# A residual of conditioned 1x1 products whose transfers move one 16 KB run per channel instead of two of 8 KB

## The reference

```python
x                 # (64, 128, 2048) float32: batch, channel, time
itok_B_0_15       # (64,) int32, 0..15
L0_cond_weights   # (16, 128, 128) float32: state, channel, feature

W = weights[condition]
return x + jnp.einsum('bct,bcd->bdt', x, W)
```

## Time and profile before

| | |
|---|---|
| median of three runs | 325.06 us |
| the profiled execution, its own time | 324.97 us |
| its span, from the first to the last instruction | 323.2 us |
| PE, DVE, POOL busy | 240.3, 146.6, 19.0 us |
| moved by DMA | 135.30 MB, 419 GB/s over the span |
| granted TensorE clock, mean | 0.928 |

### The profile page before, as it was taken

One profiled execution on the slowest core, in us unless ns is written; L12 is line 12 of the kernel. 1 busy time (PEld: TensorE's weight loads), 2 busy tenths in 40 slices (PEclk: granted clock), 3 DMA queues, 4 the chain that ended last, 5 costly groups with the idle time before them and its releaser, 6 DMA issues.

```text
span 323.2 us, 2326 instructions
## 1 busy us (share of the span) xinstructions
PE 240.3 (74%) x512; PEld 101.3 (31%) x512; DVE 146.6 (45%) x64; ACT 0.2 (0%) x1; POOL 19.0 (6%) x69
## 2 busy tenths in 40 slices
PE   0029999999999986867996869866688786878000
PEld 0014444444444432322342323322233332333000
DVE  0003766766757752555173552543545254553200
ACT  0000000000000000000000000000000000000000
POOL 0011100101001000000010000000000000000000
PEclk9999999999999998999597997999899798899755
DMA  7999999999999999999999999999999999999996
GB/s 279 382 414 422 422 425 429 428 424 430 426 428 430 425 431 426 427 431 426 429 428 427 430 425 428 430 425 430 428 427 430 426 429 428 426 430 426 429 430 284
DMA packets 17940, 135.30 MB, mean 419 GB/s; under 512 B 1042, under 2 KB 1042, under 8 KB 1554
## 3 DMA queue, kind: packets, MB, share of 16 engines
q10 hardware_dynamic: 9234, 68.16, 49.9%
q1 hardware_dynamic: 8704, 67.11, 49.7%
HBM read 68.16 MB, written 67.11 MB: 419 GB/s over the span
## 4 chain that ended last, share of the span: by engine, by line
DMA 69%; PE 20%; DVE 2%; issue 1%; ACTq 0%; POOLq 0%; DVEq 0%; ACT 0%; SPq 0%; POOL 0%
DMA out<-x_ring 59%; PE product L114 20%; DMA weight_table<-weights 6%; DMA x_ring<-x 5%; DVE x_ring L138 2%; POOLq L90 0%; ACTq L147 0%; ACTq L145 0%; DVEq L138 0%; ACT weight_table L149 0%; ACTq L144 0%; SPq L72 0%; POOLq L92 0%; SPq L84 0%; POOLq L97 0%
## 5 line engine op out<-in xcount | busy, mean ns | idle before, releaser
L114 PE MATMUL product<-x_ring,chosen_weights 128*128 (+1 forms) x512 | 240.3, 629 | 58.6 <-POOL chosen_weights L92 23.2
L138 DVE TENSOR_TENSOR x_ring<-product,x_ring 128x2048 f32 x64 | 146.6, 2291 | 154.7 <-PE product L114 154.7
L114 PEld LDWEIGHTS product<-x_ring,chosen_weights 128*128 128x128 f32 x512 | 101.3, 201 | 196.7 <-issue 196.7
L92 POOL COPY chosen_weights<-weight_table 128x128 f32 x64 | 18.8, 293 | 243.1 <-issue 125.2
L149 ACT MOVE_SHAPE weight_table<-weights x1 | 0.2, 160 | 1.4 <-PEq L166 1.4
L166 POOL MEMSET const-float32-0.0<- 128x1 f32 x1 | 0.1, 98 | 0.1
L166 POOL MEMSET const-bfloat16-1.0<- 128x1 bf16 x1 | 0.1, 101 | 0.0
L166 POOL MEMSET const-uint8-127<- 128x1 uint8 x1 | 0.1, 101 | 0.0
L166 POOL MEMSET const-float32-1.0<- 128x1 f32 x1 | 0.1, 98 | 0.0
L166 POOL BASE_LOAD x1 | 0.0, 17 | 0.2 <-issue 0.2
## 6 DMA issues: line engine op xcount, KB each, us to landing
x_ring<-x SPq DMA_DIRECT2D x32, 2048.0 KB, 16.3
out<-x_ring ACTq DMA_DIRECT2D x32, 2048.0 KB, 38.6
condition_row<-condition ACTq DMA_DIRECT2D x1, 0.2 KB
weight_table<-weights ACTq DMA_DIRECT2D x1, 0.5 KB, 18.8
```

The lines of the kernel that those rows point to most:

```text
L92: pool.tensor_copy(chosen_weights[b][:, :], weight_table[:, bass.ds(state * features, features)]).then_inc(weights_chosen, 1)
L114: last = pe.matmul(product[:, b % psum_slots, m * BANK_COLUMNS:(m + 1) * BANK_COLUMNS], chosen_weights[b][:, :], x_ring[:, bass.ds(ring_co ...
L138: dve.tensor_tensor(tile, product[:, b % psum_slots, :], tile, AluOpType.add).then_inc(sum_done, 1)
```

## The change

The launch hands `x` over as (32 groups, channel, 2 x 2048) and the weights as (channel, state, feature); the output comes back in the form of `x` and is put into the old order. This regrouping is done outside the device program. Inside it, one transfer still moves a group of 2 MB, now as one run of 16 KB per channel; the weight table comes in runs of 8 KB, and is issued ahead of the indices. Each engine has one loop of 16 turns with two groups (four batches) in each, and no code ahead of it for the first turns: semaphores are raised once at the start to take the place of what the first turns needn't wait for. The ring keeps its 8 groups (`RING_TURNS` 4 x `IN_FLIGHT` 2). `chosen_weights` has four buffers instead of eight, and they are freed by DVE (`weights_free`), not by PE. `x_loaded` and `room_free` (which takes the place of `out_stored`) have two semaphores each instead of four.

```diff
-BATCHES = 2
-STEPS = 4
-RING_TURNS = 2
+GROUP = 2
+IN_FLIGHT = 2
+RING_TURNS = 4
...
-        def batches_of(tensor, turn, u):
-            first = turn * (STEPS * BATCHES) + u * BATCHES
-            return tensor[bass.ds(first, BATCHES)].rearrange("b c t -> c b t")
+        def dram_group(tensor, turn, g):
+            return tensor[bass.ds(turn * IN_FLIGHT + g, 1)].rearrange("o c t -> c (o t)")
...
-            for u in range(STEPS):
-                load(0, u)
-
-            with sp.Fori(1, RING_TURNS) as turn:
-                for u in range(STEPS):
-                    sp.wait_ge(x_loaded[u], 16 * turn)
-                    load(turn, u)
-            with sp.Fori(RING_TURNS, turns) as turn:
-                for u in range(STEPS):
-                    sp.wait_ge(x_loaded[u], 16 * turn)
-                    sp.wait_ge(out_stored[u], 16 * (turn - RING_TURNS + 1))
-                    load(turn, u)
+            for g in range(IN_FLIGHT):
+                sp.sem_inc(x_loaded[g], 16)
+                sp.sem_inc(room_free[g], 16 * RING_TURNS)
+            with sp.Fori(0, turns) as turn:
+                for g in range(IN_FLIGHT):
+                    sp.wait_ge(x_loaded[g], 16 * (turn + 1))
+                    sp.wait_ge(room_free[g], 16 * (turn + 1))
+                    sp.dma_start(ring_group(turn, g), dram_group(x, turn, g)
+                                 ).then_inc(x_loaded[g], 16)
...
+                    pool.wait_ge(weights_free, turn * per_turn + b + 1)
...
+                    pe.wait_ge(weights_chosen, turn * per_turn + b + 1)
+                    pe.wait_ge(psum_free, turn * per_turn + b + 1)
...
+                    dve.wait_ge(product_done, turn * per_turn + b + 1)
+                    dve.sem_inc(weights_free, 1)
                     dve.tensor_tensor(tile, product[:, b % psum_slots, :], tile,
-                                      AluOpType.add).then_inc(sum_done, 1)
+                                      AluOpType.add).then_inc(psum_free, 1)
...
-            def store(turn, u):
-                act.wait_ge(sum_done, turn * (STEPS * BATCHES) + (u + 1) * BATCHES)
-                act.dma_start(batches_of(out, turn, u), ring_group(turn, u)).then_inc(out_stored[u], 16)
-
+            act.dma_start(weight_table[:, :], weights.rearrange("c s d -> c (s d)")
+                          ).then_inc(table_loaded, 16)
             act.dma_start(condition_row[0:1, :], condition.rearrange("(o b) -> o b", o=1)
                           ).then_inc(condition_loaded, 16)
...
+            with act.Fori(0, turns) as turn:
+                for g in range(IN_FLIGHT):
+                    act.wait_ge(room_free[g], 16 * (turn + RING_TURNS))
+                    act.wait_ge(psum_free, turn * per_turn + (g + 1) * GROUP + psum_slots)
+                    act.dma_start(dram_group(out, turn, g), ring_group(turn, g)
+                                  ).then_inc(room_free[g], 16)
...
+    grouped = np.asarray(x).reshape(batches // GROUP, GROUP, channels, time).transpose(0, 2, 1, 3)
...
+        "weights": np.ascontiguousarray(np.asarray(L0_cond_weights).transpose(1, 0, 2)),
```

## The result

The changed kernel takes 322.87 us (median of 4 runs, 322.56 to 322.95), the kernel before 325.22 (4 runs): a ratio of 0.9916, 95% interval 0.9900 to 0.9933. That is 2.4 us less by the medians and 2.7 by the ratio, where 3.6 were forecast (321.4 us, inside the stated range of 319.2 to 324.5). The profiled execution took 322.95 us with a span of 321.2 us, 2.0 us under that of before.

A forecast was written before the change was run, and what follows sets the result against it. The prediction took the kernel as bound by DMA, 135.30 MB through 16 engines. From 324.97 us, -2.8 for longer runs and -0.8 for the weights, the other terms zero, gave 321.4 us, range 319.2 to 324.5.

The forecast's parts named there:

- Term 1: Loads of x and stores of out: 16 KB runs halve the packets, saving 5.5 ns each; -2.8 us, ends 0 and -6.0.
- Term 4: Load and store queues: two transfers in flight instead of four cost zero, each successor starting in time.
- it stays: End of the kernel: the drop (64 GB/s in 320:323.2), from an engine running behind the others, remains unchanged.
- theory A: During the experiments: slowest of 16 DMA engines sets the end, gaining nothing from longer runs; whole gain from the weights.
- Term 2: Weight table at the start: larger pieces lift the 393 GB/s of 4:20 towards 425; -0.8 us, table landing at 9.5 us.
- Term 3: Start of SP's queue: raises and loop registers delay the first load perhaps 0.3 us, covered by the weights; zero.
- two in flight run dry: Rival, chance 0.05: where only loads or only stores run, late successors leave the engines idle; 329.1 us.
- no slice under 425: Sign for two transfers in flight costing nothing: no slice of the middle falls under 425 GB/s.
- bound of 4.4 us for a successor: Hand-over between transfers: the next gets going in under 4.4 us, within the 4.9 us of one transfer alone.
- Term 5: Compute by PE and DVE: products, adds and freeing of matrices stay covered by DMA; zero.
- the runs cost nothing: Rival, chance 0.18: pace goes by bytes, 428 GB/s as before; only the weights' gain is left, 324.2 us.
- The uncorrected line: Rival, chance 0.11: full packet price from uncorrected sizes, -6.0 and -1.2 us; middle of 436 GB/s, 317.8 us.

The follow-up runs named there:

- e1: Kernel before with x and out in 16 KB runs only; weights, loops and four in flight unchanged: 323.72 us, ratio 0.9956.
- e7: Changed kernel with groups of four batches: 32 KB runs, 4 MB transfers, ring of the same size: 326.23 us, ratio 1.0032.
- e3: Changed kernel with x and out back in 8 KB runs; new weights layout, loops and two in flight stay: 324.31 us, ratio 0.9968.
- e2: Kernel before with only the weights laid channel-major, so the table comes in 8 KB runs: 324.05 us, ratio 0.9965.
- e5: Kernel before with both new layouts (16 KB runs, weights in 8 KB runs), old loops, four in flight: 322.25 us, ratio 0.9907.
- experiment 7: Two against four in flight: both layouts on old loops with two, 323.01 us; changed kernel with four again, 322.50 us; also compares last-store landings.
- e4: Changed kernel with four transfers in flight each way instead of two, ring of the same room: 322.32 us, ratio 0.9913.
- e9: Changed kernel with four in flight instead of two, measured a second time: 322.50 us, ratio 0.9908.

## Why the prediction was right, and where it was off

**What bounds it** was right: in the changed kernel DMA sets the time, and PE's clock (0.93) cost nothing. Stretches where DMA had to wait for the engines showed in e1 (54 to 60 us) and e7 (309 to 316 us).

**Term 1, the long runs (-2.8).** The mechanism was right, and its price at the engines nearly: 4.7 ns per packet saved over 65:290 (5.3 over 150:250) against 5.5 chosen, so 2.4 us for 512 packets, at 608.2 ns per 16 KB against 607.5 forecast, 431 GB/s. The 5.5 lay between 3.0 and 11.7 by choice, and that it came so near is partly luck. The time it gave was mis-sized: 1.6 us alone (e1), 1.4 us on the new loops (e3 to the changed kernel), 1.8 us on the old ones (e2 to e5). The step that failed is the silent one from the mean pace to the end: the sum gave the last engine what the mean engine saves. With two in flight, two packets of 8 KB took the last engine 3.7 ns longer than the mean (e3, 616.5 against 612.8) and one of 16 KB 6.6 ns longer (614.8 against 608.2), and it finishes alone, 3.0 us after the others. By the loss from 290 us on, the 8 KB kernels give 2.7 (before), 2.8 (e2, 391 GB/s over 32.3 us) and 2.9 us (e3, 390 over 32.2), those of 16 KB 3.0 (e1) to 4.2; by the landings (experiment 7) the last engine is 1.8 to 2.0 us behind with 8 KB, 2.1 to 2.4 with 16 KB and four in flight, 2.7 to 3.1 with two. So this step explains about 1.0 us on the new loops, where 2.4 - 1.0 is the 1.4 measured, and 0.3 us on the old ones, where 0.3 us more stay open. The 1.0 us holds what two in flight cost with packets of 16 KB, so term 4 doesn't come on top of the 1.4. The prediction's "it stays" for the drop at the end was wrong. Why one engine lags, and why more with longer packets, no run here tells, nor which of the sixteen it is; theory A, that the time gains nothing from the runs, was wrong as well.

**Term 2, the weights (-0.8)** came out at 1.3 us by the medians of e2, though its interval (0.7 to 1.5) still holds 0.8. The upper bound of 1.2, as if the small pieces cost all of the loss in 4:20, was the better reading; the rate went to 425 GB/s as forecast for e2, and to 437 in the changed kernel. The working for the table's landing was wrong: it had the two queues alternate from the start (9.5 us), but the loads' first packet came at 5.08 us, when the table's 128 packets (1.82 to 4.97) were through. With the table issued behind the loads (e2) it landed at 11.2.

**Term 3** held: data moved no later (154 GB/s over 0:4, before 143), though SP's first load went out at 1.56 us instead of 0.80; the weights covered it, as the term said.

**Term 4, two in flight (0)** was wrong by about +0.5 us, in the direction of the rival "two in flight run dry". Its form was not that rival's: no gap of DMA shows where loads or stores run alone, and what grew is the lag of the last engine (experiment 7). Its sign, no slice under 425, wasn't met: the fourth has 388, the notch of the new loops. The bound of 4.4 us for a successor rested on an idle start; see the last section.

**Term 5, compute (0)** held: PE busy 76%, the last add 10 us ahead of the end of DMA, and no matrix waited for.

The terms as measured are about -1.6, -1.3 and +0.5: -2.4, near the -2.35 of the medians. Each is known to 0.3 us or so, so that the agreement is no finer than that. The rival "the runs cost nothing" (324.2) is excluded by e3. With it falls the reading that the 428 GB/s of the Trainium skill's copies of 16 KiB rows ("DMA: Bandwidth & Descriptors", "Latency and other measured facts") are a ceiling for loads with stores: the middle ran at 431 and with 32 KB at 434. The uncorrected line (436 GB/s, 317.8 us) is excluded too. The Trainium skill, "DMA: Bandwidth & Descriptors", section "Why small descriptors are slow (HBM only)", has about three cycles per packet, by its figures an estimate of 3.5 ns. The steps here are 4.6 and 4.7 ns per packet from 4 to 16 KB and 6 from 16 to 32 KB (605.2 ns in 65:290 of e7), so a price of that kind exists and is somewhat higher.

The better version is e5 or, in the new loops, e4: both layouts with four in flight, 322.25 and 322.32 us (e4 once more, e9: 322.50).

## What to carry to other kernels

Where DMA is the bound, each packet saved was worth a little under 5 ns on its engine, so 0.8% of the pace from 8 to 16 KB, of which 0.4 to 0.6% reached the time; for the time ends with the engine that is last, so look at the share of the last microseconds, or at the sixteen landings of the last transfer, and not at the mean rate alone. Longer runs on one queue delay a small-pieced transfer that shares the engines, since they alternated by packet here (the table landed at 28.4 us instead of 20.4): lay out the small one first. Larger transfers pay at the end, when the last group's compute is exposed: groups of 4 MB gained 0.5% in the middle and lost more behind it.

## What the runs showed of the hardware that wasn't expected

**A queue that starts beside a busy one starts late.** The first store of the changed kernel was issued at 23.33 us. Its queue q10 in 23.3:26.5 has no packet at all, and 19 in 26.5:29; the first is at 27.52. The queue lines of the two stretches:

```profile
q1 hardware_dynamic: 97, 1.33, 108.6%
...
q1 hardware_dynamic: 32, 0.52, 63.1%
q10 hardware_dynamic: 19, 0.31, 29.0%
```

So 4.2 us pass from issue to first packet, where at the start of the program, with nothing else under way, data moved within 1.2 us. The packet records of all twelve profiles show the same for the first store, 3.1 to 4.3 us (before: issued at 34.09, first packet at 37.75). It is no matter of stores: the weights of the kernel before, issued at 1.59 beside the loads, have their first 2 KB packet at 5.89, and the changed kernel's first load, issued at 1.56 beside the weights, has its first at 5.08. In 24:34 of the changed kernel DMA fell to 397 GB/s, 0.8 us lost; before, with the same delay of the first store, there is no such notch, so the delay alone doesn't explain it.
